# A mixture-of-experts kernel on one Trainium2 core: the routed down-projection in five products over 128 rows instead of six over 88

## The reference, cut to what matters

```python
x = x + 0.5 * ffn(layernorm(x))
x = x + scan_layer(layernorm(x))
x = x + 0.5 * ffn(layernorm(x))

def ffn(x):                                    # NE = 16 experts, TOP_K = 4, H = 176
    scores = sigmoid(x @ gate_w.T) + gate_b
    weights, indices = top_k(scores, 4); weights /= weights.sum(-1)
    shared = silu(x @ w1_shared) * (x @ w3_shared) @ w2_shared
    h3 = silu((x @ w1_routed[e]) * (x @ w3_routed[e]))     # per expert e, 176 wide
    routed = sum over the 4 chosen e of weight[e] * (h3 @ w2_routed[e])
    return shared + routed
```

## Time and profile before

| what | value |
|---|---|
| three timed executions | 733.77, 735.53, 735.92 us, median 735.53 |
| profiled execution, its own time | 733.44 us |
| its span, first to last instruction | 731.5 us |
| PE busy (matmuls) | 512.3 us, 70% |
| PE weight loads, beside them | 481.8 us, 66% |
| DVE busy | 470.5 us, 64% |
| POOL busy | 340.7 us, 47% |
| ACT busy | 335.1 us, 46% |
| mean granted TensorE clock | 0.845 of 2.4 GHz |
| data moved | 79.86 MB, mean 109 GB/s |

### The profile page before, as it was taken

The page is one execution under the profiler, slowest core; times in us unless marked ns, Lnnn a source line. Parts: engine busy times, 40 slices in busy tenths (PEclk is TensorE's granted clock), DMA queues, the critical chain, the costliest instruction groups (busy, mean ns, idle before and its releaser), DMA issues.

```text
span 731.5 us, 14228 instructions
## 1 busy us (share of the span) xinstructions
PE 512.3 (70%) x3442; PEld 481.8 (66%) x3443; DVE 470.5 (64%) x1317; ACT 335.1 (46%) x970; POOL 340.7 (47%) x356
## 2 busy tenths in 40 slices
PE   4824669999999990566767647799999999900000
PEld 3714559999999990355656536699999999900000
DVE  5489947777777762477764699477777777612233
ACT  3665535555555550265573444355555555400000
POOL 3369254444444416777504010544444444167774
PEclk9956789999999996688798857899999999955555
DMA  8940033444343433333202300243434434334443
GB/s 271 302 145 6 25 102 122 124 122 125 121 126 122 119 94 91 105 102 97 84 0 94 112 1 30 66 123 121 124 121 127 124 122 122 87 93 135 130 129 100
DMA packets 51433, 79.86 MB, mean 109 GB/s; under 512 B 8469, under 2 KB 37397, under 8 KB 51405
## 3 DMA queue, kind: packets, MB, share of 16 engines
q0 software_dynamic: 13824, 37.77, 19.0%
q1 hardware_dynamic: 37581, 41.75, 17.3%
HBM read 52.22 MB, written 27.26 MB: 109 GB/s over the span
## 4 chain that ended last, share of the span: by engine, by line
PE 50%; POOL 17%; issue 16%; DVE 7%; DMA 6%; ACT 3%; SPq 0%; POOLq 0%; DVEq 0%; ACTq 0%
PE bank L933 39%; POOL mamba_room L367 16%; PE bank L955 5%; PE bank L989 5%; DMA xn_scratch<-ring_f 3%; DMA ys_scratch<-ring_f 1%; DMA ring_f<-xn_scratch,tokidx 1%; DMA mamba_room<-ys_scratch,si 1%; DVE stage L748 1%; ACT w_routed L410 1%; PE bank L998 1%; DVE stage L714 1%; DVE xres L794 1%; ACT w_routed L411 1%; DMA xres<-in_x_in 0%
## 5 line engine op out<-in xcount | busy, mean ns | idle before, releaser
L933 PE MATMUL bank<-w_routed,ring_r 128*128 (+1 forms) x1920 | 313.5, 312 | 0.8 <-DVE ring_r L637 0.3
L933 PEld LDWEIGHTS bank<-w_routed,ring_r 128*128 128x128 f32 (+1 forms) x1920 | 281.8, 190 | 2.5 <-issue 2.3
L357 POOL DMA_INDIRECT ring_f<-xn_scratch,tokidx x160 | 152.5, 953 | 177.2 <-PE bank L955 172.4
L367 POOL DMA_INDIRECT mamba_room<-ys_scratch,si x128 | 125.2, 978 | 73.4 <-issue 38.1
L794 DVE SCALAR_TENSOR_TENSOR xres<-mamba_room,wk,xres 128x256 f32<-128x256 f32 (+1 forms) x128 | 53.4, 478 | 95.5 <-DMA mamba_room<-ys_scratch,si 95.5
L653 DVE TENSOR_TENSOR ring_f<-bank,ring_f 128x176 f32<-128x176 f32 x160 | 54.6, 342 | 53.5 <-ACT ring_f L438 53.4
L645 DVE TENSOR_TENSOR ring_r<-bank,ring_r 88x256 fp32r<-88x256 f32 x160 | 67.3, 421 | 33.4 <-ACT ring_r L430 28.4
L438 ACT ACTIVATE ring_f<-bank 128x176 f32<-128x176 f32 x160 | 50.8, 317 | 77.4 <-PE bank L933 77.1
L444 ACT ACTIVATE ring_f<-ring_f 128x176 f32<-128x176 f32 x160 | 56.1, 350 | 65.4 <-DVE ring_f L653 65.4
L933 PE MATMUL bank<-w_shared,ring_r 128*128 128x368 f32 (+1 forms) x384 | 79.6, 355 | 2.4 <-DVE ring_r L668 1.4
L331 POOL TENSOR_TENSOR w_routed<-raw_routed,w_routed 88x512 fp32r<-88x512 f32 (+1 forms) x31 | 43.4, 1425 | 73.3 <-ACT w_routed L411 73.3
(11 more groups left out here) (114 smaller groups left out, 504.1 us busy)
## 6 DMA issues: line engine op xcount, KB each, us to landing
ys_scratch<-ring_f SPq DMA_DIRECT2D x160, 128.0 KB, 1.7
raw_routed<-in_w13r SPq DMA_DIRECT2D x6, 704.0 KB
xn_scratch<-ring_f SPq DMA_DIRECT2D x32, 128.0 KB, 2.4
raw_routed<-in_w13r SPq DMA_DIRECT2D x8, 352.0 KB
ring_f<-xn_scratch,tokidx POOLq DMA_INDIRECT x160
raw_routed<-in_w2r SPq DMA_DIRECT2D x6, 352.0 KB
xres<-in_x_in SPq DMA_DIRECT2D x4, 512.0 KB, 5.7
mamba_room<-ys_scratch,si POOLq DMA_INDIRECT x128, 2.7
```

What stands on the lines that cost most here:

```text
L357: pool.indirect_dma_start(xg[j % UN], None, xn_dram, bass.IndirectOffsetOnAxis(ap=tokidx[:, j:j + 1], axis=0)).then_inc(s_g[j % UN], 16)
L367: pool.indirect_dma_start(cg[t % 4][:, q, :], None, ys_dram, bass.IndirectOffsetOnAxis(ap=si[:, n:n + 1], axis=0)).then_inc(s_cg[t % 4], 16)
L933: last = pe.matmul(out, a, b, start=(q == 0), stop=(q == len(terms) - 1))
```

## The change

The hidden width 176 is cut 128 + 48 instead of 88 + 88, and the second block is laid out so that one matmul does two terms:

- `hid` is 256 wide per buffer: columns 0 to 175 the product as before, 176 to 191 zero, 192 to 239 a second copy of columns 128 to 175, 240 to 255 zero. The zeros are written by four memsets in `route_end`. The copy of h2 goes to a tile of its own, `up`.
- `dve_product` is two instructions: 48 columns for the second copy, then the 176 columns.
- silu runs over 240 columns instead of 176.
- The two transposes take 128 columns each. The second gives rows 0 to 47 and, again, rows 64 to 111.
- ACT takes the high part over all 128 rows. DVE takes the low part in two instructions: rows 0 to 127 of the first block, and rows 64 to 127 of the second block in place. The second block so holds the high part in rows 0 to 63 and the low part in rows 64 to 127.
- w2 is laid out on the host with 128 rows: block one has rows 0 to 127, block two has rows 128 to 175 at 0 to 47 and again at 64 to 111. Loads and splits of w2 go over 128 rows instead of 88.
- `pe_out` is five matmuls instead of six: three for block one, and two for block two (against the high and the low weights).

```diff
--- before.py
+++ after.py
@@ -13,6 +13,8 @@
 NT = N // P
 DC = D // P
 HC = H // 2
+HB = H - P
+HD = P + 64
 
 
 NSLOT_MAX = (N * TOPK + NE * (P - 1)) // P
@@ -89,8 +91,9 @@
         xT = [[ring_r[:, (b * 2 + h) * 256:(b * 2 + h + 1) * 256] for h in range(2)] for b in range(2)]
         hT = [[ring_r[:, 1024 + (b * 2 + h) * 256:1024 + (b * 2 + h + 1) * 256] for h in range(2)] for b in range(2)]
         xg = [ring_f[:, k * D:(k + 1) * D] for k in range(UN)]
-        hid = [ring_f[:, 1024 + b * H:1024 + (b + 1) * H] for b in range(2)]
-        yb = [ring_f[:, 1376 + b * D:1376 + (b + 1) * D] for b in range(2)]
+        hid = [ring_f[:, 1024 + b * 2 * P:1024 + (b + 1) * 2 * P] for b in range(2)]
+        up = [stage[1][:, 512 + b * H:512 + (b + 1) * H] for b in range(2)]
+        yb = [ring_f[:, 1536 + b * D:1536 + (b + 1) * D] for b in range(2)]
 
 
         ring_h = ring_f[:, :].bitcast(f16)
@@ -277,13 +280,13 @@
             def load_experts(g):
                 e = slice(2 * g, 2 * g + 2)
                 sp.dma_start(raw_routed[g][:, :, 1, 0:W13], w13r_d[e].rearrange("e p c -> p e c")).then_inc(s_we[g], 16)
-                sp.dma_start(raw_routed[g][0:HC, :, 1, W13:WE], w2r_d[e].rearrange("e p c -> p e c")
+                sp.dma_start(raw_routed[g][:, :, 1, W13:WE], w2r_d[e].rearrange("e p c -> p e c")
                              ).then_inc(s_we[g], 16)
 
             def load_late(e):
                 lo = raw_routed[e // 2][:, e % 2, 1, :]
                 sp.dma_start(lo[:, 0:W13], w13r_d[e]).then_inc(s_wf[e - MAMBA_E], 16)
-                sp.dma_start(lo[0:HC, W13:WE], w2r_d[e]).then_inc(s_wf[e - MAMBA_E], 16)
+                sp.dma_start(lo[:, W13:WE], w2r_d[e]).then_inc(s_wf[e - MAMBA_E], 16)
 
             def xn_out(f, t):
                 sp.wait_ge(s_xn, f * NT + t + 1)
@@ -334,7 +337,7 @@
             def low_expert(e, n):
 
                 pool.wait_ge(s_whi, n)
-                low(e, HC, slice(W13, WE)).then_inc(s_wlo, 1)
+                low(e, P, slice(W13, WE)).then_inc(s_wlo, 1)
                 if e in POOL_UP:
                     low(e, P, slice(0, W13)).then_inc(s_wlo, 1)
 
@@ -408,7 +411,7 @@
                     act.wait_ge(s_ht, f * STEPS + NT - 2)
                 raw = raw_routed[e // 2][:, e % 2, 1, :]
                 act.activation(w_routed[:, e, 0, 0:W13], raw[:, 0:W13], ACT.Copy)
-                act.activation(w_routed[0:HC, e, 0, W13:WE], raw[0:HC, W13:WE], ACT.Copy).then_inc(s_whi, 1)
+                act.activation(w_routed[:, e, 0, W13:WE], raw[:, W13:WE], ACT.Copy).then_inc(s_whi, 1)
 
             def deviation(n, tt):
                 act.wait_ge(s_ln, n + 1)
@@ -427,7 +430,7 @@
                     n, b = base + i * UN + c, c % 2
                     act.wait_ge(s_ht, n + 1)
                     act.wait_ge(s_y, n - 1)
-                    act.activation(hT[b][0][0:HC, :], p_hT[b][0:HC, 0:2 * P], ACT.Copy).then_inc(s_hhi, 1)
+                    act.activation(hT[b][0], p_hT[b][:, 0:2 * P], ACT.Copy).then_inc(s_hhi, 1)
                 return stage
 
             def act_first(base):
@@ -435,13 +438,13 @@
                     n, b = base + i * UN + c, c % 2
                     act.wait_ge(s_h, n + 1)
                     act.wait_ge(s_ht, n - 1)
-                    act.activation(hid[b], p_h[b][:, H:2 * H], ACT.Copy).then_inc(s_a, 1)
+                    act.activation(up[b], p_h[b][:, H:2 * H], ACT.Copy).then_inc(s_a, 1)
                 return stage
 
             def act_silu(base):
                 def stage(i, c):
                     act.wait_ge(s_m, base + i * UN + c + 1)
-                    act.activation(hid[c % 2], hid[c % 2], ACT.Silu).then_inc(s_s, 1)
+                    act.activation(hid[c % 2][:, 0:HD + HB], hid[c % 2][:, 0:HD + HB], ACT.Silu).then_inc(s_s, 1)
                 return stage
 
             def xs_high(f, t):
@@ -642,15 +645,17 @@
                 def stage(i, c):
                     b = c % 2
                     dve.wait_ge(s_hhi, base + i * UN + c + 1)
-                    dve.tensor_tensor(hT[b][1][0:HC, :], p_hT[b][0:HC, 0:2 * P], hT[b][0][0:HC, :].bitcast(f32),
-                                      ALU.subtract).then_inc(s_hlo, 1)
+                    dve.tensor_tensor(hT[b][1][:, 0:P], p_hT[b][:, 0:P], hT[b][0][:, 0:P].bitcast(f32), ALU.subtract)
+                    rest = hT[b][0][64:P, P:2 * P]
+                    dve.tensor_tensor(rest, p_hT[b][64:P, P:2 * P], rest.bitcast(f32), ALU.subtract).then_inc(s_hlo, 1)
                 return stage
 
             def dve_product(base):
                 def stage(i, c):
                     b = c % 2
                     dve.wait_ge(s_a, base + i * UN + c + 1)
-                    dve.tensor_tensor(hid[b], p_h[b][:, 0:H], hid[b], ALU.mult).then_inc(s_m, 1)
+                    dve.tensor_tensor(hid[b][:, HD:HD + HB], p_h[b][:, P:H], up[b][:, P:H], ALU.mult)
+                    dve.tensor_tensor(hid[b][:, 0:H], p_h[b][:, 0:H], up[b], ALU.mult).then_inc(s_m, 1)
                 return stage
 
             def dve_slot_out(f, base):
@@ -779,6 +784,9 @@
                 dve.wait_ge(s_ted, f + 1)
                 dve.wait_ge(s_pkd, (f + 1) * NT)
                 dve.tensor_scalar(te[:, :], p_te, float(NE - 1), None, ALU.min)
+                for b in range(2):
+                    dve.memset(hid[b][:, H:HD], 0.0)
+                    dve.memset(hid[b][:, HD + HB:2 * P], 0.0)
                 dve.tensor_copy(tokidx[:, :], p_tok).then_inc(s_rt, 1)
 
             def combine(f, i, c):
@@ -974,9 +982,14 @@
                     w = routed_weights(c)
                     pe.wait_ge(s_hlo, n + 1)
                     pe.wait_ge(s_yo, n - 1)
-                    mm3(p_y[b][:, 0:D], [(hT[b][0][0:HC, q * P:(q + 1) * P], hT[b][1][0:HC, q * P:(q + 1) * P],
-                                          w(HC, 0, W13 + q * D, D), w(HC, 1, W13 + q * D, D)) for q in range(2)]
-                        ).then_inc(s_y, 1)
+                    hi, lo = hT[b]
+                    for q, (a, v) in enumerate([(hi[:, 0:P], w(P, 0, W13, D)),
+                                                (lo[:, 0:P], w(P, 0, W13, D)),
+                                                (hi[:, 0:P], w(P, 1, W13, D)),
+                                                (hi[:, P:2 * P], w(P, 0, W13 + D, D)),
+                                                (hi[:, P:2 * P], w(P, 1, W13 + D, D))]):
+                        last = pe.matmul(p_y[b][:, 0:D], a, v, start=(q == 0), stop=(q == 4))
+                    last.then_inc(s_y, 1)
                 return stage
 
             def pe_ht(f, base):
@@ -985,9 +998,9 @@
                     pe.wait_ge(s_s, f * NS + i * PE_UN + c + 1)
                     if isinstance(i, int) and c < 2:
                         pe.wait_ge(s_hlo, n - 1)
-                    for q in range(2):
-                        last = pe.transpose(p_hT[b][0:HC, q * P:(q + 1) * P], hid[b][:, q * HC:(q + 1) * HC], ident)
-                    last.then_inc(s_ht, 1)
+                    pe.transpose(p_hT[b][:, 0:P], hid[b][:, 0:P], ident)
+                    pe.transpose(p_hT[b][:, P:2 * P], hid[b][:, P:2 * P], ident
+                                 ).then_inc(s_ht, 1)
                 return stage
 
             def turn_x(f, t):
@@ -1156,7 +1169,10 @@
 
     w13 = np.concatenate([a["L0_ffn_w1_routed"], a["L0_ffn_w3_routed"]], axis=2)
     w13r = np.ascontiguousarray(w13.reshape(NE, DC, P, 2 * H).transpose(0, 2, 1, 3)).reshape(NE, P, W13)
-    w2r = np.ascontiguousarray(a["L0_ffn_w2_routed"].reshape(NE, 2, HC, D).transpose(0, 2, 1, 3)).reshape(NE, HC, W2C)
+    w2r = np.zeros((NE, P, 2, D), np.float32)
+    w2r[:, :, 0] = a["L0_ffn_w2_routed"][:, 0:P]
+    w2r[:, 0:HB, 1] = w2r[:, 64:64 + HB, 1] = a["L0_ffn_w2_routed"][:, P:H]
+    w2r = w2r.reshape(NE, P, W2C)
     w13s = np.concatenate([a["L0_ffn_w1_shared"], a["L0_ffn_w3_shared"], a["L0_ffn_gate_w"].T], axis=1)
     w13s = np.ascontiguousarray(w13s.reshape(DC, P, GS).transpose(1, 0, 2)).reshape(P, DC * GS)
     w2s = np.ascontiguousarray(a["L0_ffn_w2_shared"].reshape(2, HC, D).transpose(1, 0, 2)).reshape(HC, W2C)
```

## The result

The changed kernel takes 746.61 us (median of 5, 742.89 to 747.56) against 735.53 us (median of 5, 733.77 to 738.66). The ratio is 1.014, with an interval of 1.010 to 1.018: slower by 11 us, between 7.6 and 13. The forecast was 742.3 us, 6.8 us slower.

A forecast was written before the change was run, and what follows sets the result against it. PE was taken to bound the slot stages, with a loop of ACT and DVE becoming longer after the change. 4.6 + 2.2 = 6.8 us gave 740.2 against the profiled execution, 742.3 us on the median; range 717.5 to 749.

The forecast's parts named there:

- PE's own step: Slot stages: with one of six down-projection matmuls gone, PE's time per step falls from 2.13 to 2.01 us.
- The ring: Slot stages: ACT and DVE loop of product, silu, high part, low part, low part of x; from 1.71 to 2.16 us.
- fixed part: All of the ACT and DVE loop except the two low-part instructions: 0.34 + 0.13 + 0.38 + 0.30 + 0.41 = 1.56 us.
- forecast pair: The two 128-column low-part instructions on DVE, taken without overlap: 0.60 us, between bounds of 0.42 and 0.66.
- The steady part of the stages: Both slot stages: 154 steps go from 2.13 to 2.16 us each, +4.6 us.
- Loads and splits of w2: Start: four larger loads ahead of POOL's last tile's write cost +2.2 us, 0 if larger transfers move better; splits cost 0.
- Fill and drain: Ends of the slot stages: about 0.4 us more latency per slot, 0.12 us saved on each of three last down-projections; 0.
- The low parts 0.29 to 0.30 us apart: Sign in the slot stages: the two low-part instructions start that far apart, the x part as far behind the second.
- PE waiting at the hidden products for the low part of x: Sign in the slot stages: PE waits there once per step for DVE, about 0.15 us.
- PE is busy some 93% instead of 98: Sign in the slot stages: PE's busy share falls, with the transposes of line 989 every 2.16 us.
- POOL's last tile 2 us later: Sign in the start of the kernel: POOL's last tile comes 2 us later.
- the first rival: Slot stages: the low-part instructions overlap and PE stays the last, step 2.01 us, 719.2 us in all; chance 0.22.

The follow-up runs named there:

- the version with the low part in rows 0 to 63: Changed kernel with its second low-part instruction on rows 0 to 63 of the second block instead of 64 to 127; 721.27 us, ratio 0.977 to the kernel before.
- the row split: Kernel before with its low-part instruction over rows 0 to 87 split into rows 0 to 63 and 64 to 87; 758.70 us, ratio 1.028.

## Why the prediction was right, and where it was off

**PE's own step.** Right: 2.13 - 0.12 = 2.01 us; the version with the low part in rows 0 to 63 runs at 2.00. Rows cost nothing that shows: weight loads of the five products over 128 rows take 188 ns, and the products are 0.12 us apart.

**The ring.** Right in every member to 0.03 us. Forecast fixed part 1.56 us, measured 0.34 + 0.12 + 0.36 + 0.31 + 0.40 = 1.53; forecast pair 0.60, measured 0.63; sum forecast 2.16, measured 2.16. The two small errors cancel. The choice of no overlap for a start at partition 64 was the one that decided the sign, and the runs show it: the start partition alone separates the step of 2.00 from that of 2.16 us, and the split at row 64 of the kernel before costs 21 us where a second instruction from partition 0 costs 3. Of the two reasons given for it only the start partition holds: the version with the low part in rows 0 to 63 also writes over the tile that it reads, and it overlaps. The Trainium skill, page "VectorE: DVE Perf Modes", section "Two Vector instructions with no wait between them", states this hold; the traces agree, with 0.31 and 0.32 us against 0.21 and 0.20. What it costs comes from the runs: the 0.08 us of overlap and a gap of 0.01 to 0.03 us, each time the start changes, so twice per step.

**The steady part of the stages.** Forecast 4.6 us, measured 2 x 2.6 = 5.2.

**Loads and splits of w2.** Forecast 2.2 us, measured alone 2.4 with an interval of 0.4 to 4.3. The time bears the term out as far as that interval goes, but not its mechanism. It supposed that the larger loads delay POOL's last tile. The last tile comes at 32.15 to 32.94 us in the seven profiled kernels with 128 rows of w2, and at 32.56, 32.96 and 35.37 us in the three with 88. From 0 to 36 us the DMA engines moved 305 to 314 GB/s in the seven and 277 to 288 in the three; the kernel before and the changed one:

```profile
0.00:36.00 36.00, 22.99 (x123) 20.36 (x125) 18.38 (x68) 17.32 (x55) 12.07 (x23) 1.00 0.91 285
```

```profile
0.00:36.00 36.00, 24.44 (x128) 21.99 (x129) 18.28 (x68) 18.19 (x55) 12.79 (x23) 1.00 0.92 313
```

So more was moved in the same time, which is the case for which the prediction had put 0. Where the 2.4 us lie stays open. POOL's split keeps its time over 128 rows (1.28 us for the last one), as costed, and the four memsets take 0.07 us each, hidden.

**Fill and drain.** This term failed: I put it at 0, since the longer latency of a slot and the shorter down-projections seemed to cancel. From the first gather to the first gather of the results the first stage takes 182.8 us before and 185.9 now, the second 181.6 and 186.6: +8.1 us. The steady part explains 5.2 of them, and 2.9 lie in fill and drain. In the second layer 1.9 of them come after the last high part (5.5 us before, 7.35 now), where the first write of results on the chain takes 3.23 us, while the first one on the chain before took 2.39; most writes at the end of both stages take 1.7. Whether that write is longer because of the change wasn't tested.

**What nobody changed.** Between the results' first gather and the second layer's first gather the profiled executions differ by 2.6 us (183.2 and 185.8 us), and most of that in the stretch up to the start of the second layer, which holds combining and scan layer: 110.8 us before, 112.9 in the changed kernel, 111.6 to 115.4 in the eight experiments. The mean granted clock there goes along only roughly: 0.78 at 110.8 us, 0.75 to 0.77 from 111.6 to 112.9, 0.74 at 114.2, 115.0 and 115.4. The two with the fastest slot stages lose 4 us there, but the row split, with the slowest, loses 3.4 too. The cause stays open.

**How the sum came about.** The spans of the two profiled executions differ by 9.6 us: -0.3 up to the first gather, 5.2 in the steady part, 2.9 in fill and drain, 2.6 between the results' first gather and the second layer's, -0.9 after the last results' first gather (rounded, so they add up to 9.5). The traces thus confirm the term that decided the sign. That the forecast of 742.3 came within 4.3 us of 746.61 is in part luck: it had 2.2 us for loads of which these two traces show nothing, and nothing for the 5.5 us of fill, drain and the stretch between.

**The signs foretold.** The low parts 0.29 to 0.30 us apart: measured 0.31 and 0.32. PE waiting at the hidden products for the low part of x: it does, in the 47 steps counted above. "PE is busy some 93% instead of 98": wrong as a sign, since the matmul rows show 97%, and only the weight loads (from 97% to 90% of the stretch) show the wait. POOL's last tile 2 us later: wrong, it comes at 32.22 us, where it came at 32.96.

**A reading that proves less than it seemed.** The prediction says that PE bounds the kernel because the chain inside a stage "never leaves PE". It doesn't leave PE in the middle of the changed kernel's stage either, where the ring sets the step. What holds for the kernel before is the other sign it gives: the ring waits 0.35 to 0.42 us for PE in each step, and its weight loads fill all of the 150 us.

**Why it went the way of the forecast and not of the first rival.** The rival needed the pair to hold DVE under 0.45 us. It is 0.63 in the changed kernel and 0.41 in the version with the low part in rows 0 to 63, which came out at 721.3 us where the rival had 719.2. So the rival described that kernel rightly, a little helped by luck: its slot stages are shorter by 20 us, where the rival had 18.5, and 4 us are lost in the stretch that nobody changed.

## What to carry to other kernels

Before taking work from the busiest engine, sum the ring of hand-overs between the others: where it comes close to the new step, each instruction added to it costs its full start-to-start time. Don't trust a chain of waits that names one engine alone; look whether that engine's weight loads leave gaps. On DVE keep consecutive instructions at the same start partition (shown here for starts at 0 and 64); if half a tile needs a second pass, lay the data out so that this half begins at the partition where the neighbours begin. Here that exchange of two halves turned 1.4% slower into 2.3% faster.

## What the runs showed of the hardware that I had not expected

DVE's hold came out alike in the two shapes that ran: 128 columns over 64 rows and 256 columns over 24 rows both start 0.01 to 0.03 us after the end of the instruction ahead, and the instruction that returns to partition 0 is held the same way. DVE's hand-over to PE is longer than that to ACT: 0.14 us from the end of the x part to the first weight load (213.65 to 213.79; no step between 110 and 260 us has less than 0.13), against 0.03 to 0.04 us from a product's end to silu (214.02 to 214.05, and 216.51 to 216.55 before).
